# A Mamba block with an FP8 FFN on one core: loads of C moved within the first stage, two scans and a product of the second stage put into the end of the first, two loads of b put first behind it

## The reference

```python
proj = einsum('blh,eh->bel', xn, Win)            # 2 * 1024 channels
hs, gate = proj[:, :1024], proj[:, 1024:]
hs = silu(causal_conv(hs, Wconv, 4 taps) + bconv)
dt_in, Bm, Cm = split(einsum('bdl,pd->blp', hs, Wx), [128, 16, 16])
dt = softplus(dt_in @ Wdt.T + bdt)
h[t] = exp(A * dt[t]) * h[t-1] + dt[t] * Bm[t] * hs[t]     # 16 states a channel
y = (sum over states of h * Cm + hs * D) * silu(gate)
mamba = y @ Wout.T
ffn = fp8(gelu(fp8(xn) @ Wg0) * (fp8(xn) @ Wg1)) @ fp8(Wlin)
```

## Time and profile before

| | us |
|---|---|
| median of 3 runs | 1058.67 (1058.31 to 1058.89) |
| profiled execution, its own time | 1060.56 |
| its span | 1058.80 |
| VectorE busy | 994.5 (94%) |
| GpSimd busy | 913.0 (86%) |
| TensorE busy, matmuls | 910.5 (86%) |
| ScalarE busy | 832.8 (79%) |

### The profile page before, as it was taken

How to read it: one execution, slowest core, us unless ns; L and a number is a source line. 1 busy time by engine, 2 the same in 40 slices (tenths; PEclk the granted TensorE clock), 3 DMA queues, 4 the chain that set the end, 5 groups by cost and what they waited for, 6 DMA issues and landing times.

```text
span 1058.8 us, 14443 instructions
## 1 busy us (share of the span) xinstructions
PE 910.5 (86%) x4328; PEld 561.2 (53%) x4328; DVE 994.5 (94%) x1190; ACT 832.8 (79%) x1164; POOL 913.0 (86%) x512
## 2 busy tenths in 40 slices
PE   5888989577789987998799879887998798879998
PEld 4656757244445554554455556554555455445554
DVE  6887878799999999999999999999999999999996
ACT  5888987688888666898896668988866689888662
POOL 4566674899999899899999998999899989998993
PEclk9999999889889998999999979998999899999999
DMA  8678879991112129232121292221213922212101
GB/s 305 219 264 281 302 264 345 377 334 55 61 41 90 40 75 332 107 103 80 60 90 41 97 346 88 86 80 60 90 41 115 350 78 75 80 59 81 41 1 40
DMA packets 53208, 150.26 MB, mean 142 GB/s; under 512 B 5776, under 2 KB 14096, under 8 KB 50064
## 3 DMA queue, kind: packets, MB, share of 16 engines
q1 hardware_dynamic: 53136, 149.41, 40.6%
HBM read 111.37 MB, written 38.01 MB: 141 GB/s over the span
## 4 chain that ended last, share of the span: by engine, by line
DVE 32%; issue 25%; POOL 17%; ACT 11%; PE 7%; DMA 6%; SPq 1%; DVEq 1%; POOLq 0%; ACTq 0%
POOL dbu L858 11%; DVE da L1125 11%; DVE prod L1100 8%; DVE hp L1125 6%; POOL hp L1088 4%; DMA wf<-in_wffn 3%; ACT da L1019 2%; DVE conv L445 2%; PE yT L1251 2%; ACT L1008 1%; ACT L1007 1%; DVE gate_bf L1138 1%; DVE y L1108 1%; PE mm L1200 1%; DMA b_all<-bc_d 1%
## 5 line engine op out<-in xcount | busy, mean ns | idle before, releaser
L1019 ACT ACTIVATE da<-unit,neg_a 128x512 f32<-128x512 f32 x512 | 338.6, 684 | 156.9 <-DVE prod L1100 154.0
L858 POOL TENSOR_TENSOR dbu<-unit,b_head 128x1024 f32<-128x1024 f32 x192 | 450.0, 2367 | 0.0
L1125 DVE TENSOR_TENSOR_SCAN da<-da,dbu 128x512 f32<-128x512 f32 x352 | 417.9, 1218 | 1.3
L1251 PE MATMUL yT<-ident,prod 128*128 128x128 f32 x1408 | 227.7, 291 | 93.0 <-DVE prod L1100 92.2
L1251 PEld LDWEIGHTS yT<-ident,prod 128*128 128x128 f32 x1408 | 168.2, 147 | 227.7 <-DVE prod L1100 188.2
L1088 POOL TENSOR_TENSOR hp<-hp,c_head 128x512 f32<-128x512 f32 x128 | 162.7, 1271 | 50.7 <-DVE gate_bf L1141 46.1
L1125 DVE TENSOR_TENSOR_SCAN hp<-da,dbu 128x512 f32<-128x512 f32 x160 | 193.5, 1210 | 3.3 <-ACT da L1019 3.3
L1100 DVE TENSOR_TENSOR prod<-da,c_head 128x512 f32<-128x512 f32 x256 | 171.7, 671 | 0.0
L1200 PE MATMUL mm<-xn_b,w_sb 128*128 128x512 fp8e4 x512 | 143.8, 414 | 15.9 <-ACT acc L1039 12.9
L858 POOL TENSOR_TENSOR dbu<-unit,b_all 128x1024 f32<-128x1024 f32 x64 | 151.0, 2359 | 0.0
L1212 PE MATMUL mm<-xnT_b,wgate 128*128 128x512 f32 x256 | 128.8, 601 | 0.0
(11 more groups left out here) (123 smaller groups left out, 1285.8 us busy)
## 6 DMA issues: line engine op xcount, KB each, us to landing
unit<-unit_d SPq DMA_DIRECT2D x32, 768.0 KB, 4.2
unit_d<-dt_du SPq DMA_DIRECT2D x32, 512.0 KB, 2.9
wf<-in_wffn SPq DMA_DIRECT2D x12, 1024.0 KB, 7.1
c_head<-bc_d SPq DMA_DIRECT2D x24, 512.0 KB, 4.1
b_head<-bc_d SPq DMA_DIRECT2D x18, 512.0 KB, 4.9
unit_d<-hs SPq DMA_DIRECT2D x32, 256.0 KB, 6.6
w_sb<-w_d SPq DMA_DIRECT2D x64, 128.0 KB, 3.8
wgate<-in_win_gate SPq DMA_DIRECT2D x32, 256.0 KB, 2.7
```

The lines of the kernel that those rows point to most:

```text
L858: return nc.gpsimd.tensor_tensor(dbu[:, n % DBUS:n % DBUS + NS, :], twice, b_all[n // NS], ALU.mult)
L1019: nc.scalar.activation(da[n % SLOTS][:, :], unit[:, k % 2, 0, :], ACT.Exp, scale=neg_a[:, k, n:n + 1]).then_inc(da_ready, 1)
L1125: nc.vector.tensor_tensor_scan(state, da[n % SLOTS][:, :], dbu[:, n % DBUS, :], 0.0, ALU.mult, ALU.add).then_inc(scanned, 1)
L1251: ins = nc.tensor.matmul(yT[k % 2][:, t * P:(t + 1) * P], product[:, t * P:(t + 1) * P], ident[:, :], start=False, stop=last, is_transpose ...
```

## The change

Names as in the code:

- `c_head` is loaded at unit 6 of batches 2 and 3 (states 0 to 7, then 8 to 11), not in batch 4. The batch loop of `sync_a` is written out.
- The store of xnT stands behind the cast and load of the first chunk of a batch, in the last batch behind those of the second. Unit 1 of stage B is loaded at unit 4.
- `deviation` (the square root, with a table switch on either side) stands in front of the batch's first silu, with the tap of unit 1 ahead of it.
- The last tile of the next batch's xnT is copied behind the second softplus step, its low part made on GpSimd behind the second product.
- The low part of unit 7 is made on VectorE in the last two batches.
- `head_start` makes 8 states: two instructions between low parts, two behind them.
- ScalarE makes decays 0 and 1 of stage B's first unit ahead of `dtin`, and 2 and 3 behind `bc_low`; the switch to exp and log comes ahead of them. `skip_term` of unit 0 comes at unit 6. VectorE scans states 0 and 1 ahead of `bc` and multiplies state 0 by C between the first two `capped`.
- In `sync_b`, B of states 12 and 13 is loaded first, then xn8 and the FFN weights, then the rest of B and C, then the gate weights and xnT.

```diff
-EARLY = 6
+EARLY, SOON = 8, 2
@@ sync_a
-                wait(xnT_ready, b * HT + HT + 2)
-                sp.dma_start(row(xnT_d, b), xnT[:, :, :].rearrange("p k l -> p (k l)")).then_inc(xnT_stored, 16)
                 for k in range(KU):
                     if k % 3 == 0:
                         chunk(k // 3)
+                    if k == (3 if last else 0):
+                        wait(xnT_ready, b * HT + HT + 2)
+                        sp.dma_start(row(xnT_d, b), xnT[:, :, :].rearrange("p k l -> p (k l)")).then_inc(xnT_stored, 16)
...
-                    if last and k >= 2:
-                        g = k - 2
-                        sp.dma_start(c_head[:, g * NS:(g + 1) * NS, :] ...
-                    elif last:
-                        u = k
+                    if k == 6 and 1 <= b < B - 1:
+                        wait(xn_ready, 2 * b + 4)
+                        for g in range(2 * G_PER_B) if b == 1 else range(2 * G_PER_B, G_AHEAD):
+                            sp.dma_start(c_head[:, g * NS:(g + 1) * NS, :] ...
+                    if last and k in (0, 4):
+                        u = k // 4
@@ gpsimd_a
+                    if k == KU - 1 and b >= B - 2:
+                        continue
...
+                    if last and k in (3, 4):
+                        head_start(pool, (k - 3) * NS)
...
+                if last:
+                    for n in range(4, EARLY, NS):
+                        head_start(pool, n)
@@ vector_a
+                    if k == KU - 1 and b >= B - 2:
+                        dve.wait_ge(hs_hi_ready, b * KU + k + 1)
+                        dve.wait_ge(ssm_summed, b * KU + k + 1)
+                        dve.wait_ge(hs_lo_ready, b * KU + k)
+                        nc.vector.tensor_tensor(hs_lo[:, k % 2, :], hs[:, k, :], hs_hi[:, k % 2, :], ALU.subtract).then_inc(hs_lo_ready, 1)
...
+                if last:
+                    first_scans(dve)
                 dve.wait_ge(bc_low_copied, b + 1)
                 dve.wait_ge(bc_stored, b * 16 + 16)
                 nc.vector.tensor_tensor(bc[:, :], bc_ps[0:2 * N, :], bc_low[:, :], ALU.add).then_inc(bc_copied, 1)
                 capped(0)
+                if last:
+                    first_product(dve)
                 capped(1)
@@ scalar_a
+                newest_tap(b, 1)
+                if not last:
+                    deviation(b + 1)
                 nc.scalar.preload_act_table_set("silu_and_others")
...
-                    if k == 2 and not last:
-                        deviation(b + 1)
-                        nc.scalar.preload_act_table_set("silu_and_others")
...
                 if last:
-                    skip_unit(act, 0, 0)
+                    first_decays(act)
                 act.wait_ge(ssm_summed, b * KU + KU + 2)
                 nc.scalar.activation(dtin[:, :], dt_ps[:, :], ACT.Copy).then_inc(dtin_copied, 1)
                 nc.scalar.activation(bc_low[:, :], bc_ps[2 * N:4 * N, :], ACT.Copy).then_inc(bc_low_copied, 1)
-                nc.scalar.preload_act_table_set("natural_log_exp_and_others")
-                if not last:
-                    copy_tiles(b + 1, HT - 1, HT)
+                if last:
+                    later_decays(act)
+                else:
+                    nc.scalar.preload_act_table_set("natural_log_exp_and_others")
                 for k in range(KU):
+                    if k == 2 and not last:
+                        copy_tiles(b + 1, HT - 1, HT)
@@ stage_b
+        def first_decays(act):
+            act.sem_inc(prod_used, PROD.total)
+            act.sem_inc(hp_used, HP.total)
+            nc.scalar.preload_act_table_set("natural_log_exp_and_others")
+            act.wait_ge(unit_loaded[0], unit_loads(0, 0))
+            act.wait_ge(handed.proj_ready, B * KU)
+            for n in range(SOON):
+                decay(act, 0, n)
...
+        def first_scans(dve):
+            dve.wait_ge(handed.proj_ready, B * KU)
+            for n in range(SOON):
+                scan(dve, 0, 0, n)
+
+        def first_product(dve):
+            times_c(dve, 0, 0, 0)
@@ sync_b
+            load_states(0, G_AHEAD, b_all, 0, b_loaded)
             load_xn8(0)
             load_wffn(0)
+            load_states(0, G_AHEAD, c_all, N, c_loaded)
+            load_states(0, G_AHEAD + 1, b_all, 0, b_loaded)
+            load_states(0, G_AHEAD + 1, c_all, N, c_loaded)
             load_wgate(0)
             load_xnT(0)
-            for g in range(G_AHEAD, G):
-                load_states(0, g, b_all, 0, b_loaded)
-                load_states(0, g, c_all, N, c_loaded)
```

More of the change, by code:

```diff
@@ L151, in _ @@
         def _(dve):
-            first.vector(dve)
+            first.vector(dve, second.first_scans, second.first_product)
             second.vector(dve)
@@ L156, in _ @@
         def _(act):
-            first.scalar(act, second.skip_term)
+            first.scalar(act, second.first_decays, second.later_decays, second.skip_term)
             second.scalar(act)
@@ L329, in body @@
                                  ).then_inc(b_head_loaded, 16)
-            run_batches(sp, body)
+            for b in range(B):
+                body(b, b == B - 1)
             for stored in (xnT_stored, xn8_stored):
@@ L369, in body, with low_tile @@
                         ins.then_inc(xn_ready, 1)
-                if not last:
[L371 to L375, removed]
+                if last:
+                    for n in range(4, EARLY, NS):
+                        head_start(pool, n)
+                def low_tile(h):
+                    pool.wait_ge(xnT_ready, (b + 1) * HT + h + 1 + 2)
+                    nc.gpsimd.tensor_tensor(xnT_lo[:, h, :], xnT[:, h, :], xnT_hi[:, h, :], ALU.subtract).then_inc(lo_ready, 1)
+                if not last:
+                    for h in range(HT - 1):
+                        low_tile(h)
                 for k in range(KU):
@@ L378, in body, with vector_a @@
                     nc.gpsimd.tensor_tensor(dt_du[:, k % DTS, 1, :], dt_du[:, k % DTS, 0, :], hs[:, k, :], ALU.mult).then_inc(du_ready, 1)
+                    if k == 1 and not last:
+                        low_tile(HT - 1)
             for b in range(B):
                 body(b, b == B - 1)
-        def vector_a(dve):
+        def vector_a(dve, first_scans, first_product):
             links = [0]
@@ new lines, in later_decays, with times_c @@
+        def later_decays(act):
+            for n in range(SOON, SLOTS):
+                decay(act, 0, n)
+        def times_c(dve, b, k, n):
+            slot = PROD.slot(k, n)
+            dve.wait_ge(scanned, (b * KU + k) * N + n + 1)
+            dve.wait_ge(prod_used, PROD.slot_left(b, k, n))
+            if k == 0 and (n % NS == 0 or n - 1 not in OWN[k]):
+                dve.wait_ge(c_loaded[n // NS], b * 16 + 16)
+            nc.vector.tensor_tensor(prod[:, slot, :], da[n % SLOTS][:, :], c_all[n // NS][:, n % NS, :], ALU.mult).then_inc(prod_ready, 1)
@@ L991, in body @@
                 first = opening and k == 0
-                for n in range(N):
+                for n in range(SLOTS if first else 0, N):
                     if n == GELU and 1 <= k <= FFN_UNITS:
@@ L1018, in body @@
                         act.wait_ge(*state_left((u - 1) // KU, before, n - SLOTS + N))
[L1019 to L1020 removed]
+                    decay(act, k, n)
                     if n == FP8_MADE and 1 <= k <= FFN_UNITS:
```

72 lines of the change are left out of this document (34 added, 38 removed).

## The result

| | before | after |
|---|---|---|
| median, same chip (4 runs each) | 1058.78 | 1071.78 |
| lowest and highest | 1058.31, 1061.25 | 1069.81, 1072.75 |
| profiled execution, its span | 1058.8 | 1067.8 |
| stage A until the last `dt` | 205.40 | 215.19 |
| third scan | 208.89 | 215.86 |

A forecast was written before the change was run, and what follows sets the result against it. VectorE was taken to bound the kernel from 206.07 to 1052 us, with every engine partly idle in stage A before. Terms 1.6 + 1.0 - 1.2 - 3.8 + 2.0 - 1.7 - 2.8 + 1.5 = -3.4 gave 1055.3 us, range 1051.2 to 1058.8.

The forecast's parts named there:

- First silu: Stage A: root's table switches delay each batch's first silu; +1.6 us in batch 1, 0 in batch 2, +1.0 in batch 3.
- Last tile's copies: Softplus steps of three batches: copies moved behind the second softplus bring the first `dt` earlier; net -1.2 us.
- The end of each batch: Batches 2 to 4: no chunk wait at unit 4, low part faster on VectorE; -1.5, -1.8 and -0.5, sum -3.8 us.
- C in batches 2 and 3: C loads ahead of step-size stores make `dt` 4 wait about 1 us in both batches; +2.0, bounds 0 and 4.8.
- a rival: Batches 2 and 3: transfers take it back, `dt` 4 waits 2.4 us, +2.8, 1058.1 us; chance 0.20.
- the rival of 0.08: The "TensorE cools" rival: exposed switches and half clock in stage A, 1064.5 us; chance 0.08.
- TensorE cools: Stage A: switches exposed whole in three batches (+5.8), clock falls in two more (+3.4), 1064.5 us; chance 0.08.
- Batch 4's 1.68 wait: Last batch: first product follows first `dt`, its store lands in time and `dt` number 4's wait goes; -1.7 us.
- Two scans and a product: Work leaving VectorE's full stretch gives -2.8 us; late FFN results and decays in unit 0 give back +1.5.
- my three signs of being wrong: No VectorE wait in unit 0, `dt` 4 waiting 2 us or more, or stage A ending later than 206.

The follow-up runs named there:

- port_wait: Kernel after, with GpSimd making the inputs of states 4 to 7 only once VectorE's last cast is done: 1066.82 us (1.0061).
- low_back: Kernel after, with the low part of unit 7 of batch 4 on GpSimd again, batch 3 keeping it on VectorE: 1068.53 us (1.0086).
- c_alone: Kernel before, with C loaded at unit 6 of batches 2 and 3 and nothing else changed: 1062.01 us (1.0023).
- warm: Kernel after, with 12 more matmuls, results unused, in front of step-size product 7 in batches 2 and 3: 1069.59 us (1.0090).
- second trace of after: Unchanged kernel after, traced again from a second set of six runs: set median 1069.59 us (1.0100), traced span 1069.8.
- c_behind: Kernel after, with the C loads of batches 2 and 3 behind the step sizes' stores and the load of B: 1067.58 us (1.0073).
- root_back: Kernel after, with the square root and its two table switches behind the second silu again: 1063.69 us (1.0039).
- low3_back: Kernel after, with the low part of unit 7 of batch 3 on GpSimd again, batch 4 keeping it on VectorE: 1066.45 us (1.0070).
- three_back: Kernel after, with C in batch 4, the root behind the second silu and both low parts of unit 7 on GpSimd again: 1055.67 us (0.9965).

## Why the prediction was wrong

- **First silu.** The silu ran at 29.02, as worked out. The term was short by 1.1 in batch 1: GpSimd's low part took 1.56, since it began in VectorE's cast (29.60 to 30.82), and the clock stayed low for 5 us (32.2 to 37.1), not 3.4. Batch 3's 1.0 was measured as 1.11. In batch 2, which I set at 0, TensorE waits 0.70 where it waited 0.47, and 1.08 when the root is alone.
- **Last tile's copies.** Right: TensorE's wait at product 3 fell from 1.44 to 0.56 us, and the stretch gained 0.5 in batches 2 and 3, 0.1 in batch 1: -1.2 in sum, as forecast.
- **The end of each batch.** Right in batches 2 and 3 (-1.4, -1.6 against -1.5, -1.8), no wait for a chunk at unit 4. Wrong in batch 4: +0.7 for -1.3. I took the low part on VectorE at 0.69; it took 1.85, and 0.8 more is the half clock from 197.8 on, which I didn't have at all. Up to the first `dt` the term was to be -0.5 and came out at +2.6. With GpSimd out of the way (port_wait, low_back) it is -0.4: the term failed by the 3.0 us that VectorE's standing still for GpSimd cost.
- **C in batches 2 and 3: the step that failed.** I had the stores land 1 us late in each batch, +2.0, at most 4.8. The waits were 2.90 and 2.56. In batch 2 that is the size of the term: C alone makes `dt` 4 wait 2.28 there (c_alone), not 1, and what in my queue sum is short no run takes apart. In batch 3 C alone makes it wait 0. There I weighed C against a list of issues that I left in its old place, but the edit of the same change that saved 0.6 us at the end of the batch held the list up behind the cast, C included, by 2.3 to 2.5 us against `dtin`. I even named that delay, 0.5, in a rival, and priced it too low. And my sum has no price for TensorE's idling: another 3.3 us of half clock (warm), which only the rival of 0.08 had. Together 5.8 + 4.5, less some 1.4 us of waits at the next first `wx` product, which I put down to the root, is 8.9 instead of 2.0.
- **TensorE cools.** The rival had the right mechanism, the right side, and the wrong place: I looked for long waits at the switches, not at `dt` 4. The clock fell in two more places there, for 3.3 us (it said 3.4), and once more in batch 4. Its point of decision, 5.5 us more of bare wait than forecast, was not reached: TensorE's waits grew by 2.2 at batch 1's first `wx` product, 5.6 at `dt` 4 and 1.1 at batch 3's first `wx` product, 8.9 against the 4.6 in my sum, 4.3 more. So its 1064.5 lay nearer to the result than my forecast, but not by the sum that it was made of.
- **Batch 4's 1.68 wait.** Right, -1.6, and the first product follows the first `dt` at once, as worked out (206.34). In the second trace of after the wait is gone too, but half clock takes the gain back (11.29 from first to last `dt`, before 11.31).
- **Two scans and a product.** The -2.8 and the late FFN results (VectorE waits 0.27 and 0.84 in unit 0, 0.63 in unit 1: 1.7 against 1.5) came as written. Missed was the way there. The cast and the low part stood still for GpSimd, so the scans began at 200.59, 0.9 us behind `dtin` (199.65; in port_wait they begin 0.4 ahead of it), and the first `dt` came 1.9 later against `dtin` than before.
- The rule of the Trainium skill on descriptors in ring order ("DMA: Bandwidth & Descriptors", Queues, rings and completion order), on which I made the stores wait for C: these traces agree with it. In after the stores issued behind C land so late that `dt` 4 waits 2.90 and 2.56 us, and with C behind the stores (c_behind) both waits are gone. No run separates the ring's order from a queue that is simply full (1.04 in 112 to 116 us).
- The Trainium skill has a rule for the long cast that I did not weigh: by "SBUF — State Buffer", Who interferes with whom, a VectorE instruction with two SBUF inputs, or a cast in a two-port mode, and a GpSimd instruction that reads SBUF shut each other out, and the one that starts first holds the ports for its whole length. The trace agrees: the low part ended at 197.36 and the cast at 200.67, each about as long behind the end of one of GpSimd's two inputs (194.43 to 199.59, the first ending near 196.8 by an estimate of half of port_wait's 4.66 us) as it takes alone. The two instructions took 3.3 us longer than in port_wait (1.16 and 2.17), where I had a gain of 0.6.

With C at 2.0 and the end of batch 4 up to its first `dt` at -0.5 (it was +2.6) the ledger's 9.0 would be -1.0, against a forecast of -3.4: two terms carried 10 of the 12.4 us of error. Of my three signs of being wrong two came: `dt` 4 waits over 2 us, and stage A ends behind 206 (its last `dt` is at 215.19). VectorE's waits in unit 0, whose absence was the third, are there. The further 1.5 to 4 us of the medians lie outside these traces; the second trace shows only that other waits of TensorE can end in half clock in another execution.

## What to carry to other kernels

When a change moves loads and also shortens or lengthens the work that an issuing engine waits for, work out each load's issue time anew from both edits together; a low part that should save 0.6 us cost 3.1 here by the medians and 3.7 to 4.1 in the stretch behind it, since loads stood behind it. Price a wait of TensorE with what it costs behind it too. Before an instruction moves to VectorE, look at what GpSimd runs at that moment: the duration in a row of another place holds only beside the same neighbour.

## What the runs showed of the hardware

- Behind TensorE's waits of 4.1 to 5.5 us in batch 1 the granted clock was at 0.50 for 3 to 7 us in every trace, in some from within the wait on; behind the 1.44 us at product 3, which TensorE waits in batches 1 to 3 of the kernel before, it never fell. Between these the wait alone did not settle it. It fell behind 2.00 (root_back, 0.50 at 32 to 34 us), 2.32 (low_back, batch 2) and 2.35 (the second trace of after), and stayed at 1.00 behind 2.32 (c_alone), 2.67 (low3_back) and 2.88 (three_back). In batch 4 of after it fell behind 1.47, with 1.25 shortly ahead of it, and in the second trace, behind waits of 1.46 and 1.26 in the same places, it did not. Single runs of after scatter over 7 us, those of before over 4; that such waits are the reason fits the two traces of after and is not shown beyond them.
- A cast of 2048 columns took 1.22 us alone and 3.39 beside the second of two GpSimd instructions of 1024 columns, which took 4.66 us together when VectorE was out of their way; a 512-column subtraction 0.69 and 1.85. A 4-column multiplication of two SBUF tiles took 1.11 instead of 0.16, beside a GpSimd low part that had begun 0.2 us earlier:

```profile
35.66 1.11 DVE L426 TENSOR_TENSOR newton<-rstd 128x4 f32<-128x4 f32 x1
```
```profile
35.48 1.27 POOL L367 TENSOR_TENSOR hs_lo<-hs,hs_hi 128x512 fp32r<-128x512 f32 x1 [1.97 <-ACT hs_hi L591]
```
